# The last stores of Q and K parts move behind the next stack load, and the output bias is added in the first unit

## The reference

```python
xn = _layernorm(x)
for wl in range(16):                       # scan over wavelengths
    scores = (Q*m) @ (K*m).T * SCALE       # m = cos(phase)[wl], per head
    scores = scores * cos(KERR * scores**2)
    acc += softmax(scores) @ V * iw[wl]
attention = acc / 16 @ Wo + bo             # Q, K, V = xn @ W + b
expert = softmax(xn @ gate_w.T)[e] * (relu(xn @ w1[e] + b1[e]) @ w2[e] + b2[e])   # e: best expert, if it has room
out = x + attention + expert
```

## Time and profile before

| | |
|---|---|
| median of 3 runs | 1809.99 us (1807.09, 1809.99, 1810.4) |
| profiled execution | 1809.65 us, span 1807.9 us |
| ScalarE busy | 1726.9 us (96%) |
| VectorE busy | 1526.0 us (84%) |
| TensorE busy | 1490.7 us (82%), mean granted clock 0.986 of full speed |
| GpSimd busy | 157.6 us (9%) |

### The profile page before, as it was taken

One profiled execution on the slowest core, in us unless ns is written; L12 is line 12 of the kernel. 1 busy time (PEld: TensorE's weight loads), 2 busy tenths in 40 slices (PEclk: granted clock), 3 DMA queues, 4 the chain that ended last, 5 costly groups with the idle time before them and its releaser, 6 DMA issues. The chain is left out here.

```text
span 1807.9 us, 45710 instructions
## 1 busy us (share of the span) xinstructions
PE 1490.7 (82%) x20014; PEld 942.5 (52%) x20014; DVE 1526.0 (84%) x2554; ACT 1726.9 (96%) x533; POOL 157.6 (9%) x168
## 2 busy tenths in 40 slices
PE   4797888777899999999997787777787787778877
PEld 2364544544556666656664454444455555445555
DVE  8445887889898888988888999999988998898785
ACT  3699999999999999999999999999999999999995
POOL 6200111110000000000000131332000000000000
PEclk9799999999999999999999999999999999999998
DMA  6000111000011110111000000000000000000001
GB/s 207 21 15 15 37 49 43 23 25 15 22 36 42 42 43 20 31 36 43 22 22 15 18 12 25 23 25 19 15 2 15 15 15 15 15 15 2 8 13 31
DMA packets 44999, 50.07 MB, mean 28 GB/s; under 512 B 6725, under 2 KB 37359, under 8 KB 44799
## 3 DMA queue, kind: packets, MB, share of 16 engines
q1 hardware_dynamic: 42463, 42.91, 7.5%
q0 software_dynamic: 2048, 4.20, 0.7%
q10 hardware_dynamic: 288, 0.00, 0.0%
HBM read 30.96 MB, written 15.73 MB: 26 GB/s over the span
## 5 line engine op out<-in xcount | busy, mean ns | idle before, releaser
L1044 ACT ACTIVATE Pr<-T 128x4096 f32<-128x4096 f32 x482 | 1694.3, 3626 | 17.7 <-PE bank L924 16.9
L924 PE MATMUL bank<-Pr,Vst 128*32 128x256 f32 x15424 | 936.7, 383 | 249.6 <-ACT Pr L1044 140.9
L924 PEld LDWEIGHTS bank<-Pr,Vst 128*32 128x32 f32 x15424 | 520.2, 110 | 546.8 <-issue 343.8
L866 DVE COPY T<-bank 128x512 f32<-128x512 f32 x252 | 172.4, 684 | 82.9 <-PE bank L860 82.9
L850 DVE TENSOR_REDUCE negmax<-bank 128x2 f32<-128x512 f32 x256 | 164.1, 681 | 30.1 <-PE bank L844 28.7
L1015 PE MATMUL bank_b<-terms,ident 128*128 128x128 f32 x1024 | 150.3, 280 | 0.8 <-DVE terms L1003 0.7
L965 DVE SCALAR_TENSOR_TENSOR d_mantissa<-d_mantissa 128x1024 f32<-128x1024 f32 x108 | 147.0, 1361 | 0.0
L968 DVE SCALAR_TENSOR_TENSOR shared<-shared,d_scaled 128x1024 f32<-128x1024 f32 x108 | 140.0, 1297 | 0.0
L1015 PEld LDWEIGHTS bank_b<-terms,ident 128*128 128x128 f32 x1024 | 130.3, 192 | 16.0 <-issue 9.1
L971 DVE SCALAR_TENSOR_TENSOR shared<-d_mantissa,shared 128x1024 f32<-128x1024 f32 x108 | 132.0, 1222 | 2.9
L963 DVE SCALAR_TENSOR_TENSOR shared<-d_mantissa 128x1024 f32<-128x1024 f32 x108 | 130.9, 1212 | 0.0
(11 more groups left out here) (175 smaller groups left out, 911.1 us busy)
## 6 DMA issues: line engine op xcount, KB each, us to landing
Ks<-qk_parts SPq DMA_DIRECT2D x31, 288.0 KB
Qs<-qk_parts SPq DMA_DIRECT2D x93, 96.0 KB
work<-in_L_ffn_w_dram SPq DMA_DIRECT2D x16, 256.0 KB, 3.5
qk_parts<-Pr SPq DMA_DIRECT2D x8, 384.0 KB, 2.7
qk_parts<-work SPq DMA_DIRECT2D x8, 384.0 KB, 2.8
dispatched<-T SPq DMA_DIRECT2D x5, 512.0 KB, 4.9
region<-dispatched SPq DMA_DIRECT2D x8, 320.0 KB, 3.5
expert_out<-work SPq DMA_DIRECT2D x8, 320.0 KB, 2.4
```

Of the source, the lines that this page charges most:

```text
L866: nc.vector.tensor_copy(T[par][:, ds(p * BANK, BANK)], sc_bank[rr][:, :]).then_inc(sc_read, 1)
L924: ins = nc.tensor.matmul(bank[VC * j:VC * (j + 1), half * SEQ:(half + 1) * SEQ], Vst[par][:, at:at + VC], moving, start=opens and half == ...
L1044: nc.scalar.activation(Pr[n % RING][:, :], T[par][:, :], ACT.Exp, scale=scales[u % 2][w]).then_inc(exp_done, 1)
```

## The change

SyncE: the loop now runs for u = 2, 3 and 4. In each turn the stack of u + 2 is loaded first; then the last piece of the unit before is stored (piece 3 in the turn of u = 3, piece 7 in that of u = 4, with the wait for all stores behind it), then, for u below 4, three pieces; then come the rows. GpSimd: the four bias adds stand in a function of their own, `pool_output_bias`, which runs behind the staging of V for units 0 and 1; `pool_combine` waits for them and no longer has an add of its own in front.

```diff
+            def pool_output_bias(pool):
+
+                pool.wait_ge(xn1_ready, SIDE_TILES)
+                for c in range(CHUNKS):
+                    b = base[:, c * CH:(c + 1) * CH, :]
+                    nc.gpsimd.tensor_tensor(b, b, bo_s[:, :].unsqueeze(1).to_broadcast([P, CH, D]), ALU.add).then_inc(biased, 1)
...
             def pool_combine(pool, c):

                 s = slice(c * CH, (c + 1) * CH)
-                nc.gpsimd.tensor_tensor(base[:, s, :], base[:, s, :], bo_s[:, :].unsqueeze(1).to_broadcast([P, CH, D]),
-                                        ALU.add).then_inc(pool_comb, 1)
+                pool.wait_ge(biased, CHUNKS)
                 pool.wait_ge(gathered[c], 16 * CH)
                 nc.gpsimd.tensor_tensor(got[:, s, :], got[:, s, :], over(r[:, 0, s], D), ALU.mult).then_inc(pool_comb, 1)
-                pool.wait_ge(pool_comb, 2 * (c + 1))
+                pool.wait_ge(pool_comb, c + 1)
                 nc.gpsimd.tensor_tensor(base[:, s, :], base[:, s, :], got[:, s, :], ALU.add).then_inc(base_ready, 1)
...
                 for u in range(2):
                     stage_v(pool, u, u)
+                pool_output_bias(pool)
...
-                for u in range(2, 4):
+                for u in range(2, 5):
                     j = (u - 2) * NQ_SIDE
                     sp.wait_ge(sc_made, pair_no(u, 0))
                     load_stack(sp, u + 2, u % 2)
-                    sp_side1(sp, j, j + NQ_SIDE - 1)
+                    if u > 2:
+                        sp_side1(sp, j - 1, j)
+                    if u < 4:
+                        sp_side1(sp, j, j + NQ_SIDE - 1)
                     load_rows(sp, u + 2, u % 2)
-                    sp_side1(sp, j + NQ_SIDE - 1, j + NQ_SIDE)
-                for u in range(4, EU):
+                for u in range(5, EU):
                     unit(u, u % 2)
```

More of the change, by code:

```diff
@@ L518, in attention_and_experts @@
                 "route", "gate_in", "gate_exp", "mask_ready", "index_ready"))
-            scattered, pool_comb, base_ready = asem("scattered"), asem("pool_comb"), asem("base_ready")
+            scattered, pool_comb, base_ready, biased = asem("scattered"), asem("pool_comb"), asem("base_ready"), asem("biased")
             gathered = [asem(f"gathered{c}") for c in range(CHUNKS)]
```

## The result

The changed kernel takes 1794.51 us (median of 4 runs, 1793.29 to 1794.97), beside 1809.91 us for the kernel before (4 runs): a ratio of 0.9917, 95% interval 0.9900 to 0.9934. The forecast was 1796.3 us. The profiled execution takes 1794.94 us, 14.71 less than that of before, where the sum had 13.54.

What follows compares the result with a forecast made beforehand. ScalarE's exponentials and its waits for TensorE's products were taken to bound the kernel. From 1809.65 us, -3.73 - 4.30 - 6.74 + 1.23 made 1796.11, stated as 1796.3 us; range 1793.5 to 1800.5, widened to 1803.

Steps and rivals of the forecast that it cites:

- the sum: Whole kernel: -3.73 - 4.30 - 6.74 + 1.23 = -13.54 us from the profiled 1809.65 us, making 1796.11 us.
- What bounds the kernel: ScalarE: time is its exponentials plus its waits between first and last, 16.9 us in 15 places, all released by TensorE's products.
- Stores 3 and 7: Units 3 and 4: stack loads issued ahead of these stores close ScalarE's waits, 3.73 + 4.30 = 8.03 us gained.
- what was named as late next: Unit 3: with the load's wait gone, the second products end at 240.4, 0.7 us before ScalarE needs them.
- The adds out of units 17 to 20: Units 17 to 20: without the bias add, VectorE's lateness falls under 3.07 us and four ScalarE waits go, 6.74 us gained.
- The adds in the first unit: First unit: four adds on GpSimd hold VectorE's split of the maxima, costing 1.23 us; copies out of PSUM cost 0.
- A: Units 3 and 4: the loads gain nothing, another wait keeps the products where they are; 1804.1 us, chance 0.04.
- C: Units 17 to 20: GpSimd's gain and sum operations hold VectorE as long as before; 1802.9 us, chance 0.05.
- B: First unit: the adds also hold the copies out of PSUM, up to 9.3 us; 1804.2 us, chance 0.06.
- D: Unit 3: store 3 lands late and VectorE waits for it; slower, 1814.3 us for a 33 us landing, chance 0.02.
- E: First unit and units 17 to 20: B and C together; 1810.9 us, no change, chance 0.05.

Runs made afterwards that it cites:

- e1: Kernel before with only SyncE's new order of loads and stores, the bias adds staying in units 17 to 20: 1800.98 us.
- e2: Changed kernel with SyncE's loop of before, so only the bias adds move to the first unit: 1802.82 us.
- e4: Changed kernel with only the load of unit 5's stack ahead of its store; store 7 again precedes the load of unit 6's stack: 1799.1 us.
- e5: Changed kernel with one more bias add in each of the four combines, behind the wait for the gathers: 1793.36 us.
- e6: Changed kernel with two more bias adds in each of the four combines, behind the wait for the gathers: 1802.19 us.
- e7: Changed kernel with store 3 put behind store 4 as well, so that it goes out later still: 1794.62 us.
- e8: Changed kernel as it is, run again on one chip beside a version with later first-unit adds: 1794.51 us.

## Why the prediction was right

*What bounds the kernel.* Right: of the 14.71 us by which the profiled time fell, 16.9 - 3.4 = 13.5 are ScalarE's listed waits for the products, and 0.9 more came with them, as told below.

*Stores 3 and 7.* Right, mechanism and size: -8.18 us by the trace and -8.4 us in e1, for 8.03. The load is issued 9.3 us ahead of the store instead of behind it, and what was named as late next, the second products, ended at 240.97, where ScalarE's next exponential starts at 241.82: 0.8 us in time, for 0.7 worked out. Those products lost their second 1.6 us (3.54 to 1.93) along with the wait; between 241 and 245 us the granted clock had been 0.57 before and is 1.00 after. So of the 3.73 us at unit 3, 1.6 came from the slower products behind the late load.

*The adds out of units 17 to 20.* Right in mechanism: who holds whom came out as laid out, down to L977 held for 1.1 us (worked out: 1.3) and a later operation on two SBUF inputs for 1.2 (up to 1.4). The two stretches make 2.3 us, within the 2.2 to 2.7 of lateness worked out; at the unit's end 0.97 was left, as two waits for TensorE that the undisturbed unit has (0.53 and 0.63 us) are not there. The term was undersized: it measured 7.45 us, for 6.74. What was wrong is the upper end, "no more than 6.74 us, as ScalarE is busy otherwise": a wait costs more than the idle time that is listed. Exponentials overlap. The page of the changed kernel has them busy for 1693.5 us with a mean of 3652 ns:

```profile
L1050 ACT ACTIVATE Pr<-T 128x4096 f32<-128x4096 f32 x482 | 1693.5, 3652 | 4.2 <-PE bank L930 3.4
```

That is 1693.5 / 482 = 3.51 us for each, so about 0.14 us of one lies beside the next, and a wait between two breaks that. The timeline of the kernel before agrees, in the row behind that of unit 17:

```profile
1159.75 52.82 ACT L1044 ACTIVATE Pr<-T 128x4096 f32<-128x4096 f32 x15 [1.72 <-PE bank L924]
```

This exponential starts 1159.75 - 1105.20 = 54.55 us after the one 15 places earlier, with one wait of 1.72 us between; without a wait, in the changed kernel, 15 take 15 x 835.23 / 238 = 52.64. So a listed 1.72 us costs 1.91, and four such cost some 0.7 us more than is listed. The broken overlap is the greater part of that; the last few hundredths of each are not explained. The 0.15 us beyond 8.03 at units 3 and 4 is of the same kind, though it wasn't followed up.

*The adds in the first unit.* Right by the trace: +1.25 us for 1.23, with the copies out of PSUM untouched. The Trainium skill (SBUF — State Buffer, Who interferes with whom) counts casts among the operations that can need the shared ports, and the trace agrees: the cast itself stood, 1.43 us for 0.17, and the operations behind it ran free. That the size was met to 0.02 us is luck. The wait was 1.70, 1.71, 1.45, 1.15, 1.14, 1.46 and 1.01 us in the kernels with this place of the adds (changed, e2, e4, e5, e6, e7, e8), and two things set it. The cast took 1.43 and 1.44 us in the first two and 1.17 or 1.18 in the others, as GpSimd and VectorE come to that point by separate ways. And the products behind it took 3.64 us in four of them, as in the kernel before, but 3.33, 3.32 and 3.20 in e5, e6 and e8. The first line is of the changed kernel, the second of e8:

```profile
67.64 3.64 PE L930 MATMUL bank<-Pr,Vst 128*32 128x256 f32 x32
67.53 3.20 PE L930 MATMUL bank<-Pr,Vst 128*32 128x256 f32 x32
```

In these three the granted clock from 67 to 71 us was 0.54, 0.54 and 0.61 of full speed, in the other four 0.50, which is the lower level, 1.2 GHz. So the adds hold the split for 1.0 to 1.3 us, and a clock that rises sooner gives back up to 0.4.

*The rivals.* A and C fall with the first trace, as no wait took the old places. B falls with L872 at 0.69 us beside the adds. D falls with e7, and E, which is B and C together, with both. Between the two profiled executions the sum missed 14.71 - 13.54 = 1.17 us: 0.9 us for the overlap, and 0.5 us for an earlier first exponential, 62.52 against 62.98, less 0.1 behind the last one. The start of that first exponential lies between 62.48 and 62.98 in all the kernels above, so the 0.5 us is chance. The other 0.6 us of the 1.79 between 1796.3 and 1794.51 lie between these executions and the medians.

## What to carry to other kernels

Find the one engine whose waits make up the time, and for each of its waits ask what had been asked for late or held up; here a load behind a store that had to wait, and two engines that hold each other up, were each worth the listed waits and a little more. In a queue issued in order, put what could go at once ahead of what has yet to wait. Before moving work off a shared resource, work out how much lateness the consumer forgives: the first piece taken away may be worth everything, the next nothing.

## What the hardware showed beyond that

- A GpSimd operation is held too: L783 took 2.60 us for 1.89 when VectorE's L974 was under way at its start (1067.02, for 1.22 us), and L779 or L785 took 3.24 to 3.26 with a VectorE operation served ahead of it, where e5's (L786) took 2.36 with none.
- Not only VectorE operations on two SBUF inputs are held. In e5 L960, a tensor_scalar with one SBUF tensor as input, took 2.57 us for 0.74 beside that L786. Copies out of PSUM took their 0.68 us beside GpSimd's operations.
- Who is served between two GpSimd operations isn't the same each time. In the kernel before L965 stood until two of them, which ran back to back (the second behind a wait for the gathers), were through the earlier trace rows; in e5 L978, started at 1068.47, took 2.82 us and was through before the second such operation (L784, stretched to 2.88 us, with no wait in front of it). Why wasn't tried.
- Late loads cost twice on TensorE: the wait, and products at a lower granted clock behind it. In the kernel before TensorE idled for 2.98 us until 239.88; the clock was still 1.00 of full speed from 236 to 241 us and 0.57 from 241 to 245 (the two levels are 1.2 and 2.4 GHz). Without the wait, after the change, it is 1.00 in both.
